# First mixture layer: token weights stored undivided and earlier, division moved to the weighing of results, first expert scattered without accumulation

## What is computed

```
def _L0_ffn_ref(x, Wg, W1, W2, W3):          # 8 experts, n = 4096 tokens, capacity 512
    scores = (x_flat @ Wg.T).T
    top_vals, token_idx = jax.lax.top_k(scores, capacity)
    token_w = jax.nn.softmax(top_vals, axis=-1)
    xg = x_flat[token_idx]
    h = silu(xg W1[e]) * (xg W3[e])
    y = (h W2[e]) * token_w[..., None]
    out = zeros_like(x_flat).at[token_idx.reshape(-1)].add(y.reshape(-1, c))
```

## Time and profile before

| what | value |
|---|---|
| device time, three runs | 717.76, 718.16 and 723.28 us, median 718.16 |
| span of the profiled execution | 713.3 us |
| busy shares | PE 73%, DVE 60%, ACT 47%, POOL 44% |
| first gather to the last scatter of this layer | 144.50 to 251.74 us |
| last layer | begins near 489 us |

### The profile page before, as it was taken

One profiled execution on the slowest core, in us unless ns is written; L12 is line 12 of the kernel. 1 busy time (PEld: TensorE's weight loads), 2 busy tenths in 40 slices (PEclk: granted clock), 3 DMA queues, 4 the chain that ended last, 5 costly groups with the idle time before them and its releaser, 6 DMA issues.

```text
span 713.3 us, 13599 instructions
## 1 busy us (share of the span) xinstructions
PE 518.2 (73%) x3894; PEld 382.3 (54%) x3896; DVE 426.9 (60%) x1784; ACT 332.8 (47%) x690; POOL 313.0 (44%) x329
## 2 busy tenths in 40 slices
PE   1769610378777508877899997149999999999925
PEld 1457100245544303433334444149999999999921
DVE  4789668835322238898426878883545545455447
ACT  3815510044323115454357663165666666666616
POOL 3514300067878723243001112016777667767535
PEclk9966755569978758899999998559999999999976
DMA  7401272012323350100000100021111111111155
GB/s 189 130 0 56 69 291 123 6 38 41 45 43 43 34 173 28 31 15 1 2 0 16 31 27 20 15 24 42 50 48 49 46 47 48 48 44 49 38 202 167
DMA packets 47736, 42.23 MB, mean 59 GB/s; under 512 B 15346, under 2 KB 41835, under 8 KB 47179
## 3 DMA queue, kind: packets, MB, share of 16 engines
q1 hardware_dynamic: 35770, 25.48, 11.4%
q0 software_dynamic: 10816, 15.82, 10.6%
q10 hardware_dynamic: 1104, 0.39, 0.2%
HBM read 26.23 MB, written 15.30 MB: 58 GB/s over the span
## 4 chain that ended last, share of the span: by engine, by line
PE 45%; DVE 27%; issue 11%; POOL 6%; ACT 5%; DMA 4%; ACTq 1%; DVEq 0%; POOLq 0%; SPq 0%
PE bank L1886 18%; PE bank L1907 9%; DVE st L1259 3%; POOL sum_dram L673 3%; PE bank L1695 2%; PE bank L1740 2%; PE bank L1730 2%; DVE mv L1264 2%; POOL arena L661 2%; DVE st L989 2%; ACT arena L913 1%; POOL rstd L687 1%; PE bank L1796 1%; DVE hit L1103 1%; PE bank L1896 1%
## 5 line engine op out<-in xcount | busy, mean ns | idle before, releaser
L1886 PE MATMUL bank<-arena 128*128 128x128 f32 x1136 | 140.1, 277 | 0.4 <-ACT arena L964 0.4
L1886 PEld LDWEIGHTS bank<-arena 128*128 128x128 f32 x1136 | 133.9, 194 | 0.7 <-ACT arena L964 0.7
L687 POOL TENSOR_TENSOR rstd<-ve,mhalf 128x4 f32<-128x4 f32 x40 | 48.7, 1217 | 167.7 <-DVE ve L1267 121.7
L1519 DVE TENSOR_TENSOR arena<-arena,bank 128x512 f32<-128x512 f32 x71 | 48.8, 688 | 81.4 <-PE bank L1886 81.4
L741 POOL DMA_INDIRECT y_dram<-arena,sidx x71 | 69.9, 985 | 44.4 <-DVE arena L1524 41.1
L950 ACT ACTIVATE arena<-wgu 128x1024 f32 x71 | 75.0, 1057 | 26.5 <-PE bank L1886 26.2
L733 POOL DMA_INDIRECT arena<-x3row_dram,gidx x71 | 68.8, 969 | 36.5 <-issue 20.7
L1907 PE MATMUL bank<-w,arena 128*128 x568 | 75.1, 275 | 0.0
L1907 PEld LDWEIGHTS bank<-w,arena 128*128 128x128 f32 x568 | 69.1, 192 | 0.2 <-issue 0.2
L956 ACT ACTIVATE arena<-bank 128x512 f32<-128x512 f32 x71 | 42.4, 597 | 42.7 <-PE bank L1886 42.7
L673 POOL DMA_INDIRECT sum_dram<-arena,idx x32 | 50.7, 1585 | 15.2 <-issue 7.6
(11 more groups left out here) (326 smaller groups left out, 1049.0 us busy)
## 6 DMA issues: line engine op xcount, KB each, us to landing
wgu<-in_wgu SPq DMA_DIRECT2D x1, 4096.0 KB, 12.2
wgu<-y_dram SPq DMA_DIRECT2D x8, 512.0 KB, 6.7
X<-in_x SPq DMA_DIRECT2D x8, 256.0 KB, 5.6
sum_dram<-zero POOLq DMA_DIRECT2D x8, 256.0 KB, 4.2
x1row_dram<-row SPq DMA_DIRECT2D x8, 256.0 KB, 2.4
w<-in_w SPq DMA_DIRECT2D x1, 2048.0 KB, 17.4
acc<-sum_dram SPq DMA_DIRECT2D x8, 256.0 KB, 2.9
w<-in_wd SPq DMA_DIRECT2D x1, 2048.0 KB, 10.2
```

The lines of the kernel that those rows point to most:

```text
L687: nc.gpsimd.tensor_tensor(out, ve[:, u], mhalf[:, 0:J], ALU.pow).then_inc(done, 1)
L1519: nc.vector.tensor_tensor(gl[:, m.pair], sgl[:, m.pair], bank[3 + m.pair][:], ALU.mult).then_inc(f_gated, 1)
L1886: last = nc.tensor.matmul(bank[first + m.pair][:, h * P:(h + 1) * P], wnow[:, m.pair, at_:at_ + P], xrT[:, m.ring], start=True, stop=True)
```

## The change

The weights are stored undivided: `wtok` is now the turned `ex` itself, copied out of the accumulator bank by ACT, and ACT's own queue starts the store. The division by the expert's sum moves into the weighing of results, whose instruction takes a second factor for each partition, `wst[:, 2, lap]`. PE turns `ex` ahead of the slots. The reciprocal stands behind the first two lists. The first expert's four scatters are plain writes instead of additions. POOL gets one more wait, for the stored rows, which SP's program implied before.

```
 @block.sync
-            sp.wait_ge(c_wtok, LEAD + 1)
-            sp.dma_start(x1row_dram...[:, :, D:ROWS], wtok[:]).then_inc(c_wst, 16)
 @block.gpsimd
+            pool.wait_ge(a_rowst, LEAD + 32 * CH)
             pool.wait_ge(c_wst, LEAD + 16)
...
                     pool.wait_ge(c_yw, LEAD + n + 1)
+                    if e == 0:
+                        nc.gpsimd.indirect_dma_start(sum_dram, at, yw[:, n % 8], None).then_inc(c_acc[k], 16)
+                    else:
+                        nc.gpsimd.indirect_dma_start(sum_dram, at, yw[:, n % 8], None, compute_op=ALU.add)...
 @block.scalar
             nc.scalar.activation(ex[:], srch[:], ACT.Exp, bias=base[:, 2:3]).then_inc(c_ex, 1)
+            act.wait_ge(c_mxps, LEAD + 3)
+            nc.scalar.activation(wtok[:].rearrange("p (s h) e -> p h e s", h=2),
+                                 bank[5][:, 0:2 * P].rearrange(...), ACT.Copy).then_inc(c_wtok, 1)
+            act.wait_ge(c_wtok, LEAD + 1)
+            act.dma_start(x1row_dram...[:, :, D:ROWS], wtok[:]).then_inc(c_wst, 16)
 @block.vector
-            nc.vector.tensor_tensor(ex[:], ex[:], sel[:], ALU.mult)
+            nc.vector.tensor_tensor(ex[:], ex[:], sel[:], ALU.mult).then_inc(c_post, 1)
...
             list_part(0, 1)
-            token_weights()
             list_part(1, 0)
...
             list_done(1)
+            dve.wait_ge(c_mxps, LEAD + 4)
+            ch.mark(nc.vector.reciprocal(wst[:, 2], bank[6][:, 8:16]))
+            ch.wait()
...
                     nc.vector.tensor_scalar(yw[:, o.n % 8], bank[6][:, 0:D],
-                                            xg[:, o.n % XG, D + o.lap:D + o.lap + 1], None, ALU.mult)
+                                            xg[:, o.n % XG, D + o.lap:D + o.lap + 1], wst[:, 2, o.lap:o.lap + 1], ALU.mult,
+                                            ALU.mult).then_inc(c_yw, 1)
 @block.tensor
             (counts, L1647: rank of the slots)
+            pe.wait_ge(c_post, LEAD + 3)
+            for h in range(2):
+                last = nc.tensor.transpose(bank[5][:, h * P:(h + 1) * P], ex[:, h * P:(h + 1) * P], ident[:])
+            last.then_inc(c_mxps, 1)
             pe.wait_ge(c_q, LEAD + 1)
             (slots turned, L1650)
             pe.wait_ge(c_mx, LEAD + 3)
-            for h in range(2):
-                nc.tensor.transpose(bank[5][:, h * P:(h + 1) * P], ex[:, h * P:(h + 1) * P], ident[:])
             nc.tensor.matmul(bank[6][:, 8:16], ones[:], wst[:, 1], start=True, stop=True).then_inc(c_mxps, 1)
```

More of the change, by code:

```diff
@@ L564, in _ @@
             sp.dma_start(w2[:], inp["w2"]).then_inc(s_w0, 16)
-            sp.wait_ge(c_wtok, LEAD + 1)
-            sp.dma_start(x1row_dram.rearrange("(t p) d -> p t d", p=P)[:, :, D:ROWS], wtok[:]).then_inc(c_wst, 16)
             for k in range(4):
@@ L672, in add0 @@
                     pool.wait_ge(c_yw, LEAD + n + 1)
-                    nc.gpsimd.indirect_dma_start(sum_dram, bass.IndirectOffsetOnAxis(ap=idx[:, e, k:k + 1].bitcast(U32),
-                                                                                     axis=0),
-                                                 yw[:, n % 8], None, compute_op=ALU.add).then_inc(c_acc[k], 16)
+                    at = bass.IndirectOffsetOnAxis(ap=idx[:, e, k:k + 1].bitcast(U32), axis=0)
+                    if e == 0:
+                        nc.gpsimd.indirect_dma_start(sum_dram, at, yw[:, n % 8], None).then_inc(c_acc[k], 16)
+                    else:
+                        nc.gpsimd.indirect_dma_start(sum_dram, at, yw[:, n % 8], None, compute_op=ALU.add).then_inc(c_acc[k], 16)
             gather0(0)
@@ L824, in _ @@
             nc.scalar.activation(ex[:], srch[:], ACT.Exp, bias=base[:, 2:3]).then_inc(c_ex, 1)
+            act.wait_ge(c_mxps, LEAD + 3)
+            nc.scalar.activation(wtok[:].rearrange("p (s h) e -> p h e s", h=2),
+                                 bank[5][:, 0:2 * P].rearrange("p (h e s) -> p h e s", h=2, e=E0), ACT.Copy).then_inc(c_wtok, 1)
+            act.wait_ge(c_wtok, LEAD + 1)
+            act.dma_start(x1row_dram.rearrange("(t p) d -> p t d", p=P)[:, :, D:ROWS], wtok[:]).then_inc(c_wst, 16)
             def places(e):
@@ L1185, in _ @@
             ch.wait()
[L1187 to L1194, removed]
             def compare(out, which, e, n):
```

1 line of the change is left out of this document (removed).

## The result

The changed kernel takes 714.94 us in the median of 20 runs (712.26 to 718.63), the kernel before 718.35 in its own 20 (713.68 to 723.28). The ratio, which goes by all the runs and not by the two medians (they alone would give 0.9953), is 0.9945, with an interval of 0.9924 to 0.9966, which is 2.4 to 5.5 us less. The forecast was 714.9. Two further measurements of the same kernel gave 0.9967 (0.9945 to 0.9989) and 0.9953 (0.9924 to 0.9982).

A forecast was written before the change was run, and what follows sets the result against it. The prediction took the weights' store alone to hold POOL's first gather, and everything behind to hang on gather 8. 2.71 + 0.57 = 3.28 us off the median 718.16 gave 714.9 us, own range 713.2 to 716.4.

The forecast's parts named there:

- The store: Weights' store ahead of the first gather: starts about 135.46 from ACT's queue, lands at 140.02, at most 141.15, before the list.
- The list: First list, made by DVE and PE: done at 141.52 instead of 141.74, 0.22 us earlier of DVE's 0.68.
- With the same 0.27 POOL starts at 141.79: First gather starts 0.27 us after the list, as before after the store's landing: 141.79 instead of 144.50, 2.71 us earlier.
- The first results: PE's first steps: clock rise keeps its distance to the first tile, plus or minus 1 us; weighing's second factor costs nothing.
- Rival B: PE's clock rises sooner against the tiles, giving 1 us before result 3: 713.4 us; chance 0.13.
- Plain scatters: First expert's four scatters: only the fourth lies on the path, so gather 8 starts 0.57 us sooner; bounds 0 and 1.1.
- Rival C: A plain scatter holds POOL as long as an adding one, leaving only the earlier first gather: 715.4 us; chance 0.08.
- The rest of the stage: From gather 8 on, POOL is nearly always at work and its remaining waits move along, so everything shifts whole.
- The wait in front of the last expert: POOL's 2.58 us wait at 244.61: profile names the weighing, but the code also awaits the previous expert's scatters; moves with POOL.
- Rival A: Stages behind start with PE cold again; the clock gives back 1.7 us of the gain: 716.5 us; chance 0.17.
- Rival D: ACT's queue is held by the store's 4096 pieces, delaying multiplications by place: 720.2 us if held 8 us; chance 0.03.
- The stage and the span: Stage behind shifts whole: span 713.3 becomes 710.0; wrong if the stage ends 3.3 us earlier and the span doesn't.

## Why the prediction was right, point by point

- **What bounds the start.** Right: the store alone held POOL. With the store 1.5 us ahead of the list, the list is the releaser.
- **The store.** The forecast landing was 140.02, at 6.30 from the rank matmul; measured 6.3. The copy took 0.61 and not 0.38 (the bound of 0.72 held), and began earlier than thought, since PE turned the exponentials in 0.67 without a gap behind L1646. The rule of the Trainium skill ("DMA: Bandwidth & Descriptors", section "Issuing engines are not separate DMA queues"), that transfers started by different engines run on the same DMA engines, is borne out for this transfer: 4.5 us from ACT's queue and 4.5 from SP's.
- **The list.** Forecast 0.22 earlier, measured 0.24, and 0.23 the other way round when the division was put back.
- **"With the same 0.27 POOL starts at 141.79".** This is the step that failed, the term of the sum that was mis-sized. The 0.27 was read where another of the two waits opened last. In the changed kernel it is 0.88, and the first gather gained 2.12 us, not 2.71. Writing the list's wait first gives the 0.27 back.
- **The first results.** Forecast: the clock's rise keeps its distance, up to 1 us either way. From the first gather to the fourth scatter it was 19.22 before and 19.13 after, though the rise came 9.2 us after the first gather before and 7.8 after. The bound was too wide by far: a rise 1.4 us sooner gave 0.1. Rival B (the clock helps by 1 us) had its mechanism, and not its price. The weighing with a second factor takes 0.405 instead of 0.345 us, by the view of that single line in the changed kernel (shortest, median and longest in ns, first and last start):

```profile
L1245 DVE TENSOR_SCALAR arena<-bank,arena,wst x32: 402/405/413, 151.9 to 240.3; 128x128 f32<-128x128 f32 x32
```

  It was costed at nothing, up to 0.1 on the path; 0.06 is inside.
- **Plain scatters.** Forecast 0.57 from the fourth alone; measured 0.59 (1.86 to 1.27 from the fourth scatter to gather 8), and 0.55 and 0.57 in the runs that changed nothing else. Rival C falls.
- **The rest of the stage.** From gather 8 to the last four scatters 79.03 before, 78.98 after. Everything moved whole, as forecast, except where the clock dropped while list 3 was made (two of three executions of the changed kernel), which the prediction did not foresee for this stage: it looked for a give-back by the clock only in the stages behind.
- **The wait in front of the last expert.** The prediction held that the profile's releaser might be wrong there, and the run with the waits turned round shows it: the scatters' landing it is.
- **Rival A, given back by the clock.** The stage behind varies by more than its price, and whether with a bias stays open. From the first gather of the last layer back to the first transposes of the attention layer it took 212.8 us before, 214.9 in the first execution of the change, and 213.1 to 217.9 in others whose code there is the same. The execution of the kernel before is the shortest of the fourteen there, and the traces do not exclude that some of the gain is given back. The times speak against the whole price: with 1.7 us gone some 1.1 would be left at the measured 2.8, which lies outside the intervals of two of the three measurements of the changed kernel (2.4 to 5.5 and 1.3 to 5.5) and inside that of the second (0.8 to 4.0). This spread is why single spans say nothing of 3 us. Rival D (ACT's queue held): 0.39 us of issue, nothing.
- **The stage and the span.** The prediction would be wrong if the stage ended 3.3 us earlier and the span did not. In the first execution the last scatter starts 3.84 us earlier than before (246.35 against 250.19) and the span is only 0.9 shorter, not the 3.3 that would make it 710.0. Of the 3.84, 1.03 comes from the stages ahead; behind, the attention layer took 2.1 us more, and from the first gather of the last layer to the end 0.9 more (236.1 against 235.2). One pair of executions cannot tell a give-back from this spread; the 20 runs of each kernel show the gain.
- **The total.** 2.8 us at the end of the stage by the distances; 2.4 to 5.5 by the times. The forecast of 3.3 was 0.5 too large by the step above, and the median of 714.94, right on it, is partly luck: it also rests on three runs of before whose median, 718.16, happened to lie 0.2 from that of 20. The prediction's own range of 713.2 to 716.4 is not what its bounds add up to; -1.8 and +2.0 around 714.9 are 712.9 to 716.7. The times lie inside either.

## What to carry to other kernels

Before costing a wait that goes, find the one that will open last in its place, and read the gap behind that kind of wait, not behind the old one. Where an indirect DMA of GpSimd waits for several semaphores, write the wait that opens last first: here that was worth 0.6 us in front of the first gather and 0.6 in front of the last scatters (for other instructions no run shows it). When an engine has to wait in front of its next instruction anyway, making the one ahead cheaper only lengthens that wait; of four plain scatters one counted.

## What the runs showed of the hardware that was not expected

- GpSimd started an indirect DMA 0.27 to 0.29 us after the last wait had opened when that was the one written first, and 0.86 to 0.88 us after it when it was a later one (six kernels with a first gather at 8.64 to 8.67 and three at 8.05 to 8.06, for the same list; 0.86 and 0.27 at the last four scatters). What happens in the 0.8 us, the profile does not show. That the first written wait is the one the instruction carries is inferred from the order that helped and from the missing queue row.
- A plain indirect scatter of 128 rows of 512 bytes held GpSimd for 0.97 to 1.17 us and landed 2.4 us after its start in the median of the first execution of the changed kernel, an adding one 1.55 to 1.77 and 3.3. The third plain scatter landed later in every execution, after 3.4 to 4.2 us.
- TensorE's granted clock went up and down several times within this stage in all fourteen profiled executions shown here (twelve experiments, the changed kernel and the one before). What a fall cost depended on who waited for PE: those from 61 us after the rank matmul on cost nothing in the distances, while an early one, in three executions, went with 1.3 to 1.4 us, 0.44 to 0.58 of them in POOL's wait for list 3. The early fall lasted 3.4 us and began 3.6 us after the start of gather 8, PE having waited about 0.8 us for that gather, as it also did in the first execution of the changed kernel, without that fall. In these three the rise had come 13.4 to 13.5 us ahead of gather 8, in the others, the kernel before among them, 11.3 to 12.9 us ahead. Two of the three profiled executions of the changed kernel itself show the early fall, so it may take back a part of the 2.8 us on the average; whether the change makes it likelier stays open, since one execution of the kernel before is too few to tell.
